# Extra products on TensorE behind the last attention batch, and the router rows of batch 6 three slots later

## The reference, cut to what matters

```python
x = x + mixer(layernorm(x), ...)
x = x + cross_attention(layernorm(x), ctx, ctx)
x = x + experts(layernorm(x), router_logits, gating_einsum, linear, ...)

# experts
router_input = x * rsqrt(mean(x * x) + 1e-06) * root_size * router_scale
logits = router_input @ router_logits                  # 8 per token
_, choices = approx_max_k(logits, k=2)
tokens are sorted by chosen expert; per expert:
activation = gelu(gate) * up                           # 512 -> 2 x 512
expert_outputs = activation @ linear                   # 512 -> 512
out = sum over the two choices of weight * expert_outputs * per_expert_scale
```

## Time and profile before

| | |
|---|---|
| time, median of 3 runs | 1481.68 us (1474.73 to 1482.41) |
| profiled execution, its own time | 1481.74 us |
| its span | 1479.9 us |
| TensorE busy | 1333.3 us, 90% |
| VectorE, ScalarE, GpSimd busy | 59%, 49%, 40% |
| mean granted TensorE clock | 0.945 |

### The profile page before, as it was taken

How to read it: one execution, slowest core, us unless ns; L and a number is a source line. 1 busy time by engine, 2 the same in 40 slices (tenths; PEclk the granted TensorE clock), 3 DMA queues, 4 the chain that set the end, 5 groups by cost and what they waited for, 6 DMA issues and landing times.

```text
span 1479.9 us, 22910 instructions
## 1 busy us (share of the span) xinstructions
PE 1333.3 (90%) x7672; PEld 734.5 (50%) x7672; DVE 870.6 (59%) x1819; ACT 724.2 (49%) x1390; POOL 584.9 (40%) x859
## 2 busy tenths in 40 slices
PE   6589999999999998998787778884999999999997
PEld 4456666666666665654233333332444444444443
DVE  4887887979797978757887888645111111111111
ACT  2476667767666776662676767652111111111110
POOL 2345564555455456674223345143122222222221
PEclk9899999999999999997899988875999999999999
DMA  9000000000000000000200000002343444344322
GB/s 330 12 8 6 6 7 1 12 1 12 1 11 2 8 6 8 16 1 1 97 33 33 34 33 31 29 31 72 114 128 65 121 129 129 58 129 128 58 44 29
DMA packets 40276, 73.00 MB, mean 49 GB/s; under 512 B 18529, under 2 KB 22881, under 8 KB 39137
## 3 DMA queue, kind: packets, MB, share of 16 engines
q1 hardware_dynamic: 30224, 48.10, 9.3%
q0 software_dynamic: 8736, 20.61, 7.5%
q10 hardware_dynamic: 1200, 2.82, 0.5%
HBM read 148.91 MB, written 19.99 MB: 114 GB/s over the span
## 4 chain that ended last, share of the span: by engine, by line
PE 65%; DVE 19%; issue 5%; DMA 4%; POOL 3%; ACT 3%; SPq 0%; POOLq 0%; ACTq 0%; DVEq 0%
PE work_ps L533 11%; PE gate_ps L1502 9%; PE up_ps L1502 9%; PE down_ps L1488 9%; PE work_ps L605 7%; DVE conv L814 7%; PE work_ps L538 4%; PE work_ps L627 3%; DVE maxes L1204 3%; PE work_ps L1030 2%; PE mturn_ps L538 2%; DVE mix L730 2%; PE decay_ps L1021 2%; PE decay_ps L615 2%; DMA x_sb<-x_dram 2%
## 5 line engine op out<-in xcount | busy, mean ns | idle before, releaser
L533 PE MATMUL work_ps<-xnT,w_in 128*128 128x256 f32 (+1 forms) x1216 | 301.7, 393 | 1.3 <-ACT xnT L639 0.8
L730 POOL TENSOR_TENSOR mix<-decay,cbm 128x512 f32<-128x512 f32 x128 | 183.0, 1431 | 214.4 <-ACT decay L725 177.4
L533 PEld LDWEIGHTS work_ps<-xnT,w_in 128*128 128x128 f32 (+1 forms) x1216 | 220.5, 189 | 64.1 <-issue 33.3
L721 ACT ACTIVATE decay<-decay_ps 128x512 f32<-128x512 f32 x256 | 154.3, 603 | 112.2 <-PE decay_ps L615 109.7
L1590 POOL DMA_INDIRECT out_dram<-y_out,ids x39 | 61.9, 1587 | 336.0 <-DVE row_w L1554 232.3
L1204 DVE TENSOR_REDUCE maxes<-work_ps 128x2 f32<-128x512 f32 x256 | 166.6, 683 | 44.9 <-PE work_ps L1006 44.0
L814 DVE SCALAR_TENSOR_TENSOR conv<-raw,conv_w,conv 128x256 f32<-128x256 f32 x240 | 180.5, 757 | 6.9 <-ACT conv L681 1.1
L1102 ACT ACTIVATE prob<-decay_ps 128x512 f32<-128x512 f32 x256 | 142.7, 607 | 79.9 <-PE decay_ps L1021 79.0
L1569 DVE TENSOR_TENSOR act<-gelu,up_ps 128x512 f32<-128x512 f32 x39 | 26.8, 687 | 253.9 <-PE up_ps L1502 253.9
L725 ACT ACTIVATE decay<-decay 128x512 f32<-128x512 f32 x256 | 164.1, 641 | 4.7 <-PE work_ps L533 3.0
L1502 PE MATMUL gate_ps<-w_e,xgT 128*128 x312 | 142.2, 599 | 2.0 <-ACT xgT L1519 1.6
(11 more groups left out here) (268 smaller groups left out, 1898.9 us busy)
## 6 DMA issues: line engine op xcount, KB each, us to landing
w_e<-c_experts_dram SPq DMA_DIRECT2D x39, 3072.0 KB
normed_tokens<-r_xn SPq DMA_DIRECT2D x17, 256.0 KB, 2.1
out_dram<-x_sb SPq DMA_DIRECT2D x17, 256.0 KB, 2.6
x_sb<-x_dram SPq DMA_DIRECT2D x1, 3584.0 KB, 22.4
w_in<-c_w_inT_dram ACTq DMA_DIRECT2D x1, 2560.0 KB, 12.0
w_in<-c_w_inT_dram SPq DMA_DIRECT2D x1, 2048.0 KB, 8.6
w_out<-c_w_outT_dram SPq DMA_DIRECT2D x1, 2048.0 KB, 13.6
RT<-cum_scratch SPq DMA_DIRECT2D x32, 48.0 KB
```

The costliest lines, as they stand in the source:

```text
L533: m = e.matmul(ps[0:width, at:at + L], w_in[:, k, col:col + width], xnT[b % 2][:, k, :], start=(k == 0), stop=(k == KD - 1))
L721: e.activation(decay[s % 5][:, :], decay_ps[s % 3][:, :], ACT.Relu, scale=-1.0).then_inc(piece_done[stage], 1)
L730: return e.tensor_tensor(four(mix[s % 5]), four(decay[s % 5]), cb, ALU.mult)
```

## The change

A new helper, `repeated`, issues a number of matmuls of the ones tile (stationary) by the ones tile repeated four times (moving, 512 columns) into the third `decay_ps` bank; nothing reads the result. It is called at five places on TensorE: 8 behind the last `pv` transpose, 5 behind the last logits, 11 behind the last count, 14 behind the 32 small products ahead of `turn_x(0)`, and 3 behind `turn_x(0)`. The first three stand as pieces `keep_warm` in the last slot. Separately `late` goes from 4 to 7 for batch 6.

```diff
-DMA_ONLY = {... "out_in", "c_weight_out"}
+DMA_ONLY = {... "out_in", "c_weight_out", "keep_warm"}
...
-        late = 4 if b == NB - 2 else 0
+        late = 7 if b == NB - 2 else 0
         put(f + 12, ("r_stats", b), ("r_newton", b))
         for t in range(TPB):
             put(f + 16 + late + 2 * t, ("r_xn", b, t), ("r_store", b, t))
...
-    put(f, ("attend_v", NB - 1))
+    put(f, ("attend_v", NB - 1), ("keep_warm", 0, 8))
...
-    put(f, ("c_rank", 3), ("c_count", 3), ("c_logit", 3), ...
+    put(f, ("c_rank", 3), ("keep_warm", 1, 5), ("c_count", 3), ("keep_warm", 2, 11), ("c_logit", 3), ...
...
+        def repeated(e, count):
+
+            many = m_ones[:, :].rearrange("p (o j) -> p o j", o=1).to_broadcast([P, 4, P])
+            for _ in range(count):
+                e.matmul(score_ps[2][:, :], m_ones[:, :], many, start=True, stop=True)
+
         def tensor_attention(e, piece):
             stage, *key = piece
+            if stage == "keep_warm":
+                e.wait_ge(*done("exponent", NB * N_ITEMS - 1))
+                repeated(e, key[1])
...
+            repeated(e, 14)
             turn_x(0)
+            repeated(e, 3)
             for i in range(MT):
```

More of the change, by code:

```diff
@@ L171, in mixer_slots @@
     return slots
-DMA_ONLY = {"freed", "mixed", "cum_out", "cum_in", "ctx_in", "n_out", "router_in", "first_expert", "r_store", "out_in", "c_weight_out"}
+DMA_ONLY = {"freed", "mixed", "cum_out", "cum_in", "ctx_in", "n_out", "router_in", "first_expert", "r_store", "out_in", "c_weight_out", "keep_warm"}
 def bank_use(stage, *key):
@@ L290, in attention_slots @@
         put(f, ("r_xn", NB - 1, t), ("r_store", NB - 1, t), ("out_in", NB - 1, t), ("r_keep", NB - 1, t))
-    put(f, ("c_rank", 3), ("c_count", 3), ("c_logit", 3), ("c_exp", 3), ("c_slots", 3), *[("place", c, t) for t in (14, 15) for c in range(2)])
+    put(f, ("c_rank", 3), ("keep_warm", 1, 5), ("c_count", 3), ("keep_warm", 2, 11), ("c_logit", 3), ("c_exp", 3), ("c_slots", 3), *[("place", c, t) for t in (14, 15) for c in range(2)])
     put(f, ("c_base",), ("c_spread", 0), ("c_weight", 3), ("c_weight_out", 3), ("c_spread", 1))
```

## The result

The change made the kernel 0.8% faster: the ratio of the times, after to before, is 0.9924 with a 95% interval of 0.9904 to 0.9944. The median over 12 executions is 1470.78 us (1466.12 to 1476.9). That of the kernel before, in 12 executions beside them, is 1482.05 us (1474.73 to 1492.2). Forecast was 1470.4.

A forecast was written before the change was run, and what follows sets the result against it. TensorE, busy 90%, was taken to bound the kernel through its clock, which falls near 978 us. Terms -9.1 - 0.5 - 0.6 - 0.3 - 0.8 = -11.3 from 1481.74 gave 1470.4 us, range 1464.5 to 1479.5.

The forecast's parts named there:

- Part 1: Attention's end: batch 6 rows three slots later shrink TensorE's wait and hold the clock, last `pv` transpose 9.1 us sooner.
- The `pv` transpose: Last `pv` transpose of the attention: takes 0.6 us in place of 1.08 at the upper clock, -0.5 us.
- The router of batch 7: Transposes and router products of batch 7 at the upper clock: -0.6 us, at most 0.9, since VectorE limits the second copy.
- From the count to `own_tile`: Chain to the row ids is VectorE's, and the gather waits for stored weights: 0 us gained.
- The turn: First turn ahead of the first gate: 1.11 us would become 0.60, of which -0.3 us was taken.
- The gate: First gate: 5.33 us could become 3.60 at the upper clock, -1.7; half was taken, -0.8 us.
- rival B: Clock falls all the same near 978 in the 1.07 us wait; 1478.5 us, chance 0.17.
- Rival A: Products in the tail do not hold the clock, some groups overrun, only the move pays; 1473.1 us, chance 0.20.
- Rival C: Products of ones cost as much as f32 ones, 0.86 us each, and overrun their waits; 1490.1 us, chance 0.04.
- The prediction's overrun of 1.0 us: Groups of ones at the lower clock, by the skill's price: 1.0 us beyond their waits, nearly all in the 14.
- Rival D: Everything holds, in the attention's end and the tail: -12.7 us, 1469 us or a little under, chance 0.11.

The follow-up runs named there:

- the first two experiments: Against the kernel before: rows of batch 6 later without products, ratio 0.9952; the 41 products with the rows in the old order, ratio 0.998.
- the second profile of the change: The change run again unaltered for another profiled execution, against the kernel before: median 1468.77 us, ratio 0.9911.
- the first six experiments: Against before: move only, products only, wait filled in old order; against the change: only 14 and 3, only 8, 5 and 11, groups doubled; 1471.96 to 1477.07 us.
- the second set: Kernels with the move only, products only, wait filled in the old order, and 14 and 3 only, run beside before (median 1480.51 us).

## Why the prediction was right, step by step

**Part 1** was forecast at -9.1 and is -10.8 in the traces. TensorE's work in the stretch was forecast at 10.8 us and is 10.96. The waits were the mis-sized term: 4.9 forecast, 3.0 measured (1.05 for the first `pv` copy, 0.45 for `r_xnT`, 0.69 and 0.81 at the end). The two waits for exponentials and the one for the second `pv` copy didn't come, as the router's work now fills them. Of the 10.8 us, 8.5 are the same work at the upper clock (19.49 us busy before, 10.96 after) and 2.3 are shorter waits (5.30 and 3.00). That the move alone makes this and the products don't is shown by the first two experiments.

**The `pv` transpose** was -0.5 and is -0.46: from its start to that of the next step it is 4.80 us before and 4.34 after. **The router of batch 7** was -0.6 with -0.9 as its end: from the `a_xn` transpose to the count it is 7.48 before and 6.57 after, the whole -0.9. In the second profile of the change it is 7.48 again: behind the wait of 1.98 us that the 8 leave, the `a_xn` transpose took 1.04, so this term depends on the execution. From the count to `own_tile` it is 5.04 in both: the chain there is VectorE's, as forecast. **The turn** was -0.3; from its start to the gate's it is 2.74 and 2.32, -0.4. **The gate** was -0.8, half of 1.7; it is -1.6. The half was a hedge between two outcomes, and both exist: of the nine kernels with both groups, the gate takes (start to start) 3.5 in seven, 3.95 in one and 5.2 in one, that with fills at the batch starts.

The terms come to -14.3 in the traces against -11.3. The medians differ by 11.3 all the same, with an interval of 8.3 to 14.2 us. Scatter alone may be the reason: by the change's second profile (A 18.83, B 30.39) the same places give 13.4, which lies inside. A real part may be that the clock does not always hold in the moved order. In the eleven profiles with the rows of batch 6 moved, A was 18.8 in six and 21.7 to 22.5 in five (four of these five also have work moved further ahead). In three of the five it fell in the second router product or right behind it, as here in the kernel with groups of 8, 5 and 11 only:

```profile
981.91 0.63 PE L538 MATMUL work_ps<-ident,r_xn 128*128 128x128 f32 x4
...
983.32 1.39 PE L1056 MATMUL work_ps<-w_router,r_xnT 128*128 128x8 f32 x8 [0.46 <-ACT r_xnT L1142]
...
986.76 1.93 PE L1039 MATMUL work_ps<-prob,v_aug 128*32 128x512 f32 x8
```

In the other two, those with the count later, it fell in the very wait of 1.05 us for `pv`, came back with the first `r_xn` transpose and fell again behind the router products. This is the kernel with the count alone:

```profile
983.58 1.07 PE L540 MATMUL work_ps<-ident,pv 128*128 128x128 f32 x4 [1.05 <-ACT pv L1120]
...
987.52 0.66 PE L540 MATMUL work_ps<-ident,r_xn 128*128 128x128 f32 x4
...
993.97 1.94 PE L1041 MATMUL work_ps<-prob,v_aug 128*32 128x512 f32 x8
```

So **rival B** was right that the clock can still fall, in two of eleven profiles also in the place, and wrong in the price: it took the rest to stay as before (23.1 us, 7.4 more than 15.7), but in these two the clock was back within 4 us, and in all five the falls cost 2.8 to 3.7 us of A. That before's own profile lost more there than its others do is unlikely: the kernel with the products only has the same order and the same A (29.66).

That the forecast meets the median to 0.4 us is partly luck. In the traces its terms are 3 us too small, and by the ratios the move alone is worth 7.1 us where it was forecast at 9.6, and the products 3.0 (0 is within the interval) where 1.7 were forecast. What the experiments bear out is the mechanism: the wait, the clock behind it, and the gate.

**Rival A** (the products don't hold the clock) is half true: in after the clock fell behind the router products at 1008.8, most of the groups of 5 and 11 ran at the lower level, and so did a part of the 14 (4.63 us where 14 at 0.215 are 3.0); this cost nothing here, for they stand in waits, and at the gate the clock was up. **Rival C** fell: a product takes 0.215 us at the upper clock. My value of 0.275, from the transposes, was too high by a quarter; the price in the Trainium skill ("TensorE: Matmul & The Clock Gate", Wait — 56ns, not 53.3ns?) of 0.2157 us is what the doubled groups show. The prediction's overrun of 1.0 us by the lower price there adds up to 0.9; the two kernels whose 14 began at the lower clock showed 0.4 to 0.5. **Rival D** is nearest to the traces (-12.7 against -14.3), the forecast to the medians.

## What to carry to other kernels

A wait on TensorE costs more than its length when the clock falls in it: here one of 2.7 us stood ahead of a stretch that took 24.8 us and takes 14.0 without it. Look for such a wait in the rows where the granted clock changes, and give the waiting step a later place behind work that is ready; in the traces that made 10.8 us, and filling the wait with products 3.9 (by the ratios 7.1 and 3.4, with intervals that overlap). The same move one batch ahead made 7 us more. Products that nobody reads paid in the traces mostly ahead of the dense work of the first gate (1.6 of 3.5 us), and only as many as the wait covers are free. In no median here are they set apart from none.

## What the runs showed of the hardware

The place of the clock's falls changes between executions of one instruction list, and the time follows it. Of the 33 executions of before in the second set, the fastest (1472.58 us) had a mean granted clock of 0.948 and the slowest (1489.55 us) one of 0.933. Up to the first `pv` transpose of batch 7, the programs that differ only behind it (before, the change, and the first six experiments) reached it between 969.1 and 982.2 us. The time at the lower clock from 600 to 965 us was 81.9 to 116.7 us; it was longest in the slowest, but the others don't stand in step (969.1 us with 95.6, 972.8 with 81.9). A wait of the same length cost the clock in one execution and not in another: behind the wait of 1.05 us for `pv` the transpose took 0.63 in the profile of the change and 1.07 in that of the count later. So a single profile shows whether the clock can fall at a place, not how often.
